# Eight encoder layers in a twelve-stage kernel: both residuals made by tokens on GpSimd and added by VectorE, in place of identity products on TensorE

## The reference

```
q = phi(h @ Wq + bq); k = phi(h @ Wk + bk); v = h @ Wv + bv        # phi = elu + 1, 16 heads of 8
att = (q @ (k^T v)) / (q . sum(k) + 1e-6)
xn1 = norm(att @ Wo + bo + h);              h1 = xn1 * g1 + be1
xn2 = norm(gelu(h1 @ W1 + c1) @ W2 + c2 + h1);  h  = xn2 * g2 + be2
```

## Time and profile before

| what | value |
|---|---|
| runs, median (lowest to highest) | 4205.52 us (4197.21 to 4217.93) |
| the profiled execution's own time | 4226.02 us |
| its span | 4224.6 us |
| mean granted TensorE clock | 0.843 |
| busy: PE, PEld, DVE, ACT, POOL | 82%, 59%, 57%, 42%, 16% |
| `att2` in the span | about 2204 to 3340 us |

### The profile page before, as it was taken

The page is one execution under the profiler, slowest core; times in us unless marked ns, Lnnn a source line. Parts: engine busy times, 40 slices in busy tenths (PEclk is TensorE's granted clock), DMA queues, the critical chain, the costliest instruction groups (busy, mean ns, idle before and its releaser), DMA issues. The chain is left out here.

```text
span 4224.6 us, 78458 instructions
## 1 busy us (share of the span) xinstructions
PE 3483.0 (82%) x30666; PEld 2501.6 (59%) x30666; DVE 2390.4 (57%) x8662; ACT 1773.1 (42%) x3295; POOL 662.0 (16%) x1005
## 2 busy tenths in 40 slices
PE   4688876669968779699988999999997699957884
PEld 2366653335547435355557998888886455535673
DVE  5656647651157631255547777777776555574547
ACT  0034321112235212143337888888885344412320
POOL 0000000240073420111102222222221100000000
PEclk8789977667779667699999999999998799966765
DMA  4000000012110012100000000000000000000000
GB/s 145 1 2 3 3 2 1 15 35 73 50 47 13 26 52 74 52 11 12 9 1 1 10 10 10 1 10 10 10 1 1 1 1 1 1 0 2 3 3 21
DMA packets 77400, 76.32 MB, mean 18 GB/s; under 512 B 8235, under 2 KB 65871, under 8 KB 76906
## 3 DMA queue, kind: packets, MB, share of 16 engines
q1 hardware_dynamic: 68842, 54.51, 4.4%
q0 software_dynamic: 8192, 16.79, 1.4%
HBM read 44.41 MB, written 26.87 MB: 17 GB/s over the span
## 5 line engine op out<-in xcount | busy, mean ns | idle before, releaser
L134 POOL TENSOR_SCALAR rstd<-mean_var 128x4 f32<-128x4 f32 x96 | 24.3, 253 | 1972.2 <-DVE mean_var L125 1972.2
L1932 DVE SCALAR_TENSOR_TENSOR shared_floats<-bank,L_b,shared_floats 128x512 f32<-128x512 f32 x208 | 155.7, 749 | 312.9 <-ACT shared_floats L2007 312.9
L2007 ACT ACTIVATE shared_floats<-bank,L_b 128x512 f32<-128x512 f32 x208 | 142.9, 687 | 427.7 <-PE bank L1848 427.7
L1871 PEld LDWEIGHTS bank<-ffn,shared_floats 128*128 128x128 f32 x1664 | 218.2, 194 | 143.1 <-issue 84.0
L1478 PE MATMUL bank<-shared_floats 32*128 32x32 f32 (+4 forms) x2048 | 230.0, 353 | 78.5 <-DVE shared_floats L1623 48.6
L2150 PE MATMUL bank<-layer,shared_floats 128*128 128x128 f32 x2048 | 272.8, 276 | 0.0
L2425 ACT ACTIVATE shared_floats<-bank,layer 128x256 f32<-128x256 f32 x512 | 210.4, 471 | 107.1 <-PE bank L2137 107.0
L1478 PEld LDWEIGHTS bank<-shared_floats 32*128 32x128 f32 x2048 | 181.2, 225 | 124.8 <-DVE shared_floats L1623 65.2
L1871 PE MATMUL bank<-ffn,shared_floats 128*128 128x128 f32 x1664 | 225.9, 279 | 32.7 <-DVE shared_floats L1941 32.6
L2150 PEld LDWEIGHTS bank<-layer,shared_floats 128*128 128x128 f32 x2048 | 251.9, 194 | 0.0
L1847 PE MATMUL bank<-xnT,ffn 128*128 128x512 f32 x416 | 246.4, 676 | 0.0
(11 more groups left out here) (294 smaller groups left out, 8662.5 us busy)
## 6 DMA issues: line engine op xcount, KB each, us to landing
shared_floats<-bins SPq DMA_DIRECT2D x32, 320.0 KB, 4.1
results<-shared_floats SPq DMA_DIRECT2D x32, 320.0 KB, 3.4
expert_weights<-in_dram_experts SPq DMA_DIRECT2D x32, 304.0 KB, 3.1
layer<-in_dram_layers SPq DMA_DIRECT2D x8, 902.0 KB, 5.5
bins<-zero SPq DMA_DIRECT2D x1, 5760.0 KB, 22.5
ffn<-in_ffn SPq DMA_DIRECT2D x1, 2496.0 KB
bins<-xn,f_bin_row POOLq DMA_INDIRECT x128, 2.2
results<-results,result_rows POOLq DMA_INDIRECT x128
```

The lines of the kernel that those rows point to most:

```text
L1871: m = T.matmul(k.bank[7][:, tile(t)], hid[:, tile(t)], down_w[:, tile(r)], start=False, stop=(r == ROWS2 - 1), skip_group_check=True)
L1932: V.scalar_tensor_tensor(out=act[:, :], in0=k.bank[3 + g % 2 * 2][:, :], scalar=b13[:, 2 * r + 1:2 * r + 2], in1=act[:, :], op0=ALU.add, o ...
L2007: A.activation(act[:, :], k.bank[2 + g % 2 * 2][:, :], ACT.Identity, bias=b13[:, 2 * r:2 * r + 1]).then_inc(k.sem("f2_identity"), 1)
```

## The change

Both residuals are kept by tokens, with biases as rows that are repeated on all partitions. In the weights of a layer, six rows of 128 (`g1_rows`, `be1_rows`, `c2_rows`, `g2_rows`, `be2_rows`, `next_bo_rows`) come in, and the columns `bo` and `c2` go. POOL folds `c2` into `be1` and the next layer's `bo` into `be2` once per layer (`add_rows`), and per unit makes `xn2 * g2 + be2` (`next_residual`, for the next layer) and `xn1 * g1 + be1` (`inner_residual`), two instructions each, behind the two roots of the iteration. For the first layer it adds `bo` to the normed input (`first_residuals`). DVE adds the residual to the PSUM bank and writes the sum to SBUF (`add_residual1`, `add_residual2`), where `norm_stats` and `norm_apply` now read it; it waits for its own sum before the statistics. PE's identity products L2118 and L2148 go, and so do `add_bo` and `add_c2`. The copies of h and h1 for the products stay as they are.

In `att1`, three semaphores are counted as one (`l1_parts`), and `place_values` of the first two chunks waits for the first `key_heads` and not for a memset.

```diff
@@ weights of a layer
-         "bq": 1, "bq1": 1, "bo": 1, "g1": 1, "be1": 1, "c2": 1, "g2": 1, "be2": 1, "c1": NF}
+         "g1_rows": P, "be1_rows": P, "c2_rows": P, "g2_rows": P, "be2_rows": P, "next_bo_rows": P,
+         "bq": 1, "bq1": 1, "g1": 1, "be1": 1, "g2": 1, "be2": 1, "c1": NF}
@@ att1, scalar
-            A.wait_ge(k.sem("l1_cleared"), c + 1)
+            A.wait_ge(k.sem("l1_k_heads"), 1)
@@ att2, tensor: turn_att, project_out, narrow
-            T.wait_ge(k.sem("e2_xn1"), u)
+            T.wait_ge(k.sem("e2_sum1"), u)
...
-        T.wait_ge(k.sem("e2_h_bo"), u + 1)
         for t in range(QT):
-            to = k.bank[3][:, S + t * P:S + (t + 1) * P]
-            T.matmul(to, attT[:, tile(t)], w["wo"], start=True, stop=False)
-            m = T.matmul(to, h_bo[:, tile(t)], k.ident[:, :], start=False, stop=True)
+            m = T.matmul(k.bank[3][:, S + t * P:S + (t + 1) * P], attT[:, tile(t)], w["wo"], start=True, stop=True)
...
             if u:
-                T.wait_ge(k.sem("e2_xn2"), u)
-        T.matmul(to, h1_c2[:, tile(t)], k.ident[:, :], start=True, stop=False, skip_group_check=True)
+                T.wait_ge(k.sem("e2_sum2"), u)
@@ att2, vector
+    def add_residual1(u):
+        V.wait_ge(k.sem("e2_out"), u + 1)
+        V.wait_ge(k.sem("e2_hb"), residuals_made(u))
+        V.tensor_tensor(k.sb("e2_sum1", [P, S])[:, :], k.bank[3][:, HIGH], residual(k, u), ALU.add).then_inc(k.sem("e2_sum1"), 1)
+        V.wait_ge(k.sem("e2_sum1"), u + 1)
+
+    def add_residual2(u):
+        V.wait_ge(k.sem("e2_narrow"), u + 1)
+        V.wait_ge(k.sem("e2_h1b"), u + 1)
+        V.tensor_tensor(k.sb("e2_sum2", [P, S])[:, :], k.bank[7][:, 0:S], k.sb(f"e2_h1b{u % 3}", [P, S])[:, :],
+                        ALU.add).then_inc(k.sem("e2_sum2"), 1)
+        V.wait_ge(k.sem("e2_sum2"), u + 1)
...
         if 3 <= g < U2 + 3:
-            V.wait_ge(k.sem("e2_narrow"), g - 2)
-            norm_stats(k, "e2_xn2", g - 3, k.bank[7])
-        if g < U2:
-            add_bo(g)
-        if 2 <= g < U2 + 2:
-            add_c2(g - 2)
+            add_residual2(g - 3)
+            norm_stats(k, "e2_xn2", g - 3, k.sb("e2_sum2", [P, S]))
         if 1 <= g <= U2:
-            V.wait_ge(k.sem("e2_out"), g)
-            norm_stats(k, "e2_xn1", g - 1, k.bank[3][:, HIGH])
+            add_residual1(g - 1)
+            norm_stats(k, "e2_xn1", g - 1, k.sb("e2_sum1", [P, S]))
@@ att2, gpsimd
+    def scale(xn, g_rows, to):
+        k.g.count(G.tensor_tensor(tiles(to), tiles(xn[:, :]), by_rows(g_rows), ALU.mult))
+        G.wait_ge(k.g.sem, k.g.n)
+
+    def next_residual(u):
+        w, to = layer_weights(k, u), residual(k, u + B)
+        G.wait_ge(k.sem("e2_xn2"), u + 1)
+        scale(k.sb("e2_xn2", [P, S]), w["g2_rows"], to)
+        G.tensor_tensor(tiles(to), tiles(to), by_rows(w["be2_rows"]), ALU.add).then_inc(k.sem("e2_hb"), 1)
+
+    def inner_residual(u):
+        w, to = layer_weights(k, u), k.sb(f"e2_h1b{u % 3}", [P, S])
+        G.wait_ge(k.sem("e2_xn1"), u + 1)
+        if u >= 3:
+            G.wait_ge(k.sem("e2_sum2"), u - 2)
+        scale(k.sb("e2_xn1", [P, S]), w["g1_rows"], to[:, :])
+        G.tensor_tensor(tiles(to[:, :]), tiles(to[:, :]), by_rows(w["be1_rows"]), ALU.add).then_inc(k.sem("e2_h1b"), 1)
...
             norm_rstd(k, "e2_xn1", g - 1)
+        if 3 <= g < U2 - B + 3:
+            next_residual(g - 3)
...
+        if 1 <= g <= U2:
+            inner_residual(g - 1)
@@ att2, sync
             k.nc.sync.wait_ge(k.sem("e2_hT"), (layer - 1) * B)
+            k.nc.sync.wait_ge(k.sem("e2_hb"), residuals_made(layer * B - 1))
```

More of the change, by code:

```diff
@@ L396, in encoder_layouts @@
         "own_head16": np.ascontiguousarray(feature[:, None] // HD == np.arange(H)[None, :], dtype=np.float32),
+        "L2_first_bo": rows(f["L2_attn_bo"][0]),
         "L2_final": np.concatenate([rows(f["L2_attn_gf"]), rows(f["L2_attn_bef"])], 1),
@@ L1063, in states @@
         k_tok, v_tok = k.sb("l1_k_tok", [P, CH]), k.sb("l1_v_tok", [P, BPC * P])
-        T.wait_ge(k.sem("l1_v"), c + 1)
+        T.wait_ge(k.sem("l1_parts"), 3 * c + 1)
         for b in range(BPC):
@@ L1071, in sum_heads @@
         prod = k.sb("l1_prod", [P, CH])
-        T.wait_ge(k.sem("l1_prod"), c + 1)
-        T.wait_ge(k.sem("l1_state"), c + 1)
+        T.wait_ge(k.sem("l1_parts"), 3 * c + 3)
         for t in range(TPC):
@@ L1184, in add_bias @@
         V.tensor_tensor(tiles(v_tok[:, :]), tiles(k.bank[2][:, 0:BPC * P]),
-                        k.w["L1_bv"][:, :].unsqueeze(1).broadcast_to([P, BPC, P]), ALU.add).then_inc(k.sem("l1_v"), 1)
+                        k.w["L1_bv"][:, :].unsqueeze(1).broadcast_to([P, BPC, P]), ALU.add).then_inc(k.sem("l1_parts"), 1)
     def multiply_sums(c):
@@ L1374, in att1_gpsimd @@
     for n in range(2):
-        G.memset(k.sb(f"l1_v_heads{n}", [P, 4 * CH])[:, :], 0.0).then_inc(k.sem("l1_cleared"), 1)
+        G.memset(k.sb(f"l1_v_heads{n}", [P, 4 * CH])[:, :], 0.0)
     for g in range(-2 * TPC, STEPS1 + TPC):
@@ L2061, in turned, with residual, residuals_made, by_rows @@
     return k.sb("e2_hT", [P, N])[:, u % B * S:(u % B + 1) * S]
+def residual(k, u):
+    return k.sb("e2_hb", [P, N])[:, u % B * S:(u % B + 1) * S]
+def residuals_made(u):
+    if u < B:
+        c = u // 2
+        return u + 1 + max(0, 2 * c - 4)
+    g = u - B + 3
+    return u - B + 1 + 2 * (1 + min(NC - 1, (g + 1) // 2))
+def by_rows(rows):
+    return rows.unsqueeze(1).broadcast_to([P, QT, P])
 def att2_tensor(k, s):
@@ L2365, in att2_vector @@
         if 1 <= g <= U2:
-            norm_apply(k, "e2_xn1", g - 1, k.bank[3][:, HIGH])
+            if g > 1:
+                V.wait_ge(k.sem("e2_h1b"), g - 1)
+            norm_apply(k, "e2_xn1", g - 1, k.sb("e2_sum1", [P, S]))
         if g < U2 and g % B == 10 and g // B + 1 < L2:
@@ L2455, in leave_rstd, with first_residuals, add_rows @@
         G.tensor_tensor(rstd[:, :], rstd[:, :], k.neg_half[:, 0:TPC], ALU.pow).then_inc(k.sem("e2_left_rstd"), 1)
+    def first_residuals(c):
+        G.wait_ge(k.sem("ln_xn"), s.ln0 + c + 1)
+        for half in range(2):
+            G.tensor_tensor(tiles(residual(k, 2 * c + half)), tiles(k.xn(s.t0 + c)[:, half * S:(half + 1) * S]),
+                            by_rows(k.w["L2_first_bo"][:, :]), ALU.add).then_inc(k.sem("e2_hb"), 1)
+    def scale(xn, g_rows, to):
[13 more added lines that the diff above has]
+        G.tensor_tensor(tiles(to[:, :]), tiles(to[:, :]), by_rows(w["be1_rows"]), ALU.add).then_inc(k.sem("e2_h1b"), 1)
+    def add_rows(layer):
+        w = layer_weights(k, layer * B)
+        G.wait_ge(k.sem(f"e2_layer_in{layer % 2}"), 16 * (layer // 2 + 1))
+        for to, of in (("be1_rows", "c2_rows"), ("be2_rows", "next_bo_rows")):
+            k.g.count(G.tensor_tensor(w[to], w[to], w[of], ALU.add))
+        G.wait_ge(k.g.sem, k.g.n)
     ln_rstd(k, s, 0)
+    first_residuals(0)
+    add_rows(0)
     for g in range(LEAVE + 2 * NC):
@@ L2464, in att2_gpsimd @@
             norm_rstd(k, "e2_xn1", g - 1)
+        if 3 <= g < U2 - B + 3:
+            next_residual(g - 3)
+        if g < 2 * NC - 2 and g % 2 == 0:
+            first_residuals(g // 2 + 1)
+        if 1 <= g <= U2:
+            inner_residual(g - 1)
+        if g < U2 and g % B == 10 and g // B + 1 < L2:
+            add_rows(g // B + 1)
         if g >= LEAVE and (g - LEAVE) % 2 == 0:
```

29 lines of the change are left out of this document (15 added, 14 removed).

## The result

The changed kernel takes 4437.27 us (4436.54 to 4444.46, three runs) against 4205.52 before: ratio 1.0553, 95% interval 1.0508 to 1.0598. The forecast was slower, 4250; the loss is five times the one forecast, and outside the range (4155 to 4305). The profiled execution has a span of 4435.7, 211 over the 4224.6 of before. Between the first and the last masked state of the encoder lie 1110.3 us before (2205.2 to 3315.5) and 1328.7 after (2188.5 to 3517.2), 218 more, so the loss is all there (ahead of it the changed kernel takes 17 less, behind it 9 more).

The account below looks back on a forecast made before the run. Two rings of waits bound each encoder unit at 8.14 us; ring B's 7.84 plus a clash of 0.5 to 1.0 gave a middle of 8.55, +0.41 x 113 = +46 us, put at 4250, range 4155 to 4305.

Parts of the forecast that it names:

- The two rings: Waits going round once per encoder unit: PE with ACT (8.14 us, no slack), and through the norms (0.37 slack).
- ring B: Waits through narrow, DVE's and POOL's norm work, attend and turn_att; 7.77 us before, 7.84 after without a clash.
- The additions: DVE's two new PSUM and SBUF additions, both on ring B: 0.424 us each, 0.45 with the wait.
- POOL's operations: Four products or sums of 128x256 a unit on POOL, 0.64 us each; not the bound.
- The clash at the application of xn1: POOL's next_residual starts first and holds out DVE's applications of xn1 from SBUF: +0.5 to 1.0 us a unit.
- the maps of q and k: DVE's other readers of two SBUF operands, 2.9 us behind the root; their waiting was costed at nothing.
- 8.55 at full clock: Forecast time of one encoder unit in us, the middle of 8.34 to 8.84, +0.41 over before.
- rival 4: Longer POOL operations, maps blocked too, or PE's clock lowered: 9.0 us a unit or more, +100 us; chance 0.08.
- signs of being wrong: POOL's operations over 1.45 us, ring of PE and ACT still setting the unit, or PE's clock falling mid-encoder.
- 113 units: Multiplier from unit time to whole kernel: 98 dense encoder units plus the other 30 at half weight.
- Rival 1: No clash that counts at the application of xn1: 7.84 us a unit, 4172 us; chance 0.28.
- Rival 2: DVE gets its first xn1 application in, POOL's product blocks the second: 8.14 us a unit, 4205 us; chance 0.20.

Follow-up runs that it names:

- e4_small: The changed kernel with POOL's four per-unit operations cut to 2 of 256 columns, every wait kept: 4244.74 us, ratio 0.9945.
- e7_late_mask: As e6_mask, and POOL's four operations wait until DVE has masked the next unit's state: 4241.12 us, ratio 0.9918.
- e6_mask: The changed kernel with L2279 alone made a tensor_tensor, the applications still reading SBUF: 4340.02 us, ratio 1.0144.
- e5_fill: The changed kernel with eight idle 128x128 products in PE's queue ahead of its wait for the masked state: 4416.83 us, ratio 1.0343.
- e9_first: As e6_mask, with a 0.2 us memset on POOL ahead of next_residual: 4361.37 us, ratio 1.0206.

## Why the prediction was wrong

**What bounds the kernel: right.** The two rings held. 7.84 without a clash was forecast for ring B; e4_small has 7.94 and e7_late_mask 7.89. These are means that take in longer units at the start of the window; the median from one `attend` to the next is 7.88 and 7.82. That 0.89 us less work on TensorE gives only 0.20 to 0.25 is measured.

**The additions: right.** 0.43 and 0.39 against 0.424, and DVE takes 2708.01 - 2706.44 = 1.57 from the first addition to the second statistics where 1.60 was forecast and 1.19 was before.

**POOL's operations: a little low.** 0.72 each, 0.64 forecast; its bounds (0.45 to 1.07) hold it. The 0.78 that the prediction estimates by the Trainium skill (GPSIMD Engine Reference, Elementwise — side-by-side cycle accounting) is 0.06 over where mine is 0.08 under. Its working is not shown; the 4.50 us that this section has for 2048 elements, put through the sum that made 0.64, is an estimate of (4.50 - 0.22)/8 + 0.22 = 0.76. POOL is busy 373 of 800 us, not the bound.

**The clash at the application of xn1: right in kind and size.** 1.48 for two instead of 0.60, so +0.88, in the forecast's 0.5 to 1.0. e6_mask, where it is the only clash left, has 8.77 a unit, between the forecast's 8.34 and 8.84. The rule of the Trainium skill (SBUF — State Buffer, Who interferes with whom), that a `tensor_scalar` in a two-port mode and a GpSimd instruction exclude each other for the whole instruction, the prediction could not show from a row; the trace now agrees for the application, 0.88 at most against 0.32 at least. One argument for it was mis-sized: at 512 elements in 0.55 us, 0.06 us is the time of 56 elements, not of 64.

**The step that failed: what else meets POOL's operations.** The prediction took the two applications and the maps of q and k for all that could meet them. The maps it had right: L2310 takes 0.41 to 0.43 in the whole changed kernel. L2279, `mask_state`'s second half on ring B, reads one SBUF table and a PSUM column in a `tensor_scalar`; I sorted instructions by how many SBUF operands they have and not by whether that form is held out. It cost 0.70 - 0.23 = 0.47 a unit, directly behind the delayed application and in front of the `attend` on which TensorE waits. 7.84 + 0.88 + 0.47 = 9.19, against the 9.24 of a unit at full clock and the 9.30 of e5_fill.

**And the step that priced the clock at nothing.** The forecast took 8.55 at full clock and kept a falling clock for rival 4, with a chance of 0.08; that clock was also among its signs of being wrong, and is the one that showed (0.89). With 2.0 us idle ahead of every `attend`, work behind it runs at half clock in part of the units, and much of it (`narrow`'s first half, `turn_xn1`, then `turn_att` and the second half) stands on ring B behind the wait. That makes 9.3 into 10.2. So the loss is 0.88 + 0.47 + 0.93 = 2.28 on 7.94, against the 0.20 gained. Only the first two terms test the account: with them 7.94 becomes 9.29, and e5_fill has 9.30. The third is the difference between e5_fill and the changed kernel, so the whole sum, 10.22, must come out near 10.23. The prediction's 113 units were too many: 218 us over 10.23 - 8.14 is 104.

**Rivals.** Rival 1 (no clash) is what e4_small made on purpose, at 7.94. Rival 2 did not happen, and e9_first did not make it. Rival 4 (9.0 a unit or more) is the one that came, by the clock, which it named, and by L2279, which it did not; at 10.23 the loss is more than twice its 100 us.

## What to carry to other kernels

Before work is given to an idle GpSimd, list every VectorE instruction that can run beside it, and sort them by form: here a `tensor_scalar` from an SBUF tensor waits, even with 16 columns and its scalar in PSUM, and so do two-SBUF-operand instructions; the same work from PSUM, or as a `tensor_tensor` of PSUM and SBUF, does not. Then place GpSimd's work by a wait, beside those that don't; a wait on the idle engine was the whole repair. And when a wait opens in TensorE's queue, look at the granted clock of that stretch next: here the fallen clock cost 0.93 us a unit, on top of the 1.35 of the two clashes that opened the wait.

## What the runs showed of the hardware

- An instruction of 128x16 that takes 0.23 us took 0.71 beside a GpSimd operation of 0.72, and 0.16 written as a `tensor_tensor` with its data in PSUM.
- Two VectorE applications took 1.48 us in place of 0.60 when a GpSimd operation had begun 0.14 ahead of the first; the second was held as well, by the next GpSimd operation.
- Behind a GpSimd memset, with the next GpSimd operation beginning 0.01 after the first application, they took 1.62. Which of the two held the first is not shown.
- In a loop that left TensorE idle for 2.0 us a round, 49 of 77 rounds took 10.77 to 11.10 us in place of 9.24 to 9.28, at a granted clock of 0.84 in the one looked at; with 1.46 idle a round the clock was 1.00.
- Eight added matmuls a unit made the kernel 1.8% faster (1.0343 against 1.0532, each of the kernel before on its chip), as the granted clock of the stretch went from 0.90 to 1.00.
